# Attention layers of a transformer kernel: the large projection pieces in two halves, the small pieces behind the products with v

## The chip, the cores and the metric

One core of one Trainium2 chip runs the whole kernel. The metric is the device time of one execution in microseconds (us); the kernel before takes 1481.46 us, the median of three runs (1475.09 to 1482.32).

## The reference

The reference is two layers on x of shape (8, 512, 256). Layer one is softmax attention with 16 heads of 16, biases and a head mask, a residual and a layer norm. Layer two is a pre-norm block (rms norm, rotary embedding, causal attention, residual; rms norm, a mixture of 8 experts with the top 2 of each token, residual) with a residual and a layer norm around it.

```python
attn = softmax(einsum('bqhd,bkhd->bhqk', q, k) / sqrt(16)) * head_mask      # layer 1
x = layernorm(x + einsum('bhqk,bhkd->bqhd', attn, v).reshape(b, s, 256) @ Wo.T + bo)
h = x + causal_attention(rope(rmsnorm(x, g1)))                              # layer 2
y = h + moe(rmsnorm(h, g2))                                                 # 8 experts, top 2
x = layernorm(x + y)
```

## The kernel before

The change lies in `attention_layers`, which takes about the first 890 of the 1478 us. What follows it (routing, expert tiles, the last norm) is untouched.

**Units, groups, quarters.** Both attention layers run as one pipeline of 16 units u: units 0 to 7 ("plain") are the eight batches of layer one, units 8 to 15 ("causal") those of layer two. A unit has four groups n = 4u + g of four heads, and every group has four quarters (here q0 to q3; g0 to g3 for the groups). There are lead-in and run-out groups before and after (`FIRST` to `LAST`). Every engine walks the same loop over n and quarter in an order written out by hand; semaphores alone hold them together.

**A quarter on TensorE** (the loop at the end of the tensor block): two score products (`score`, tile `ps_s`, keys by queries of group n) and two products for the row maxima (`maximum`, tile `ps_m`, of group n + 3), then one *piece*, then two more of each, and then the product of the exponentials with v (`weigh`, tile `ps_o`). In causal units a masked diagonal (`diagonals`, L843 and the 128-column products behind it) follows the piece. `ps_s` and `ps_m` have three banks each: a product waits until ScalarE's exponential (`exponential`, L987) or VectorE's maximum (`take`, L1056) three back has emptied its bank.

**Pieces.** All other work of TensorE goes through the one bank `ps_x`. The table `piece_at(n, i)` names the piece that quarter i of group n carries. Eight of a unit are large: q and k of unit u + 2 (`qk`, four pieces in g1 and g3; six matmuls of 512 columns each, L670), v of unit u + 1 (two, g0; twelve of 256 columns, L681) and the output projection of unit u - 1 (`out`, two, g2; twelve of 256, L714). The small ones are `rows` (the maxima turned by four transposes, L702; two a unit) and, for causal units, `turn` (x, eight transposes, two), `parts` (the normed x, eight transposes, two) and `logits` (the router, 24 tiny matmuls). A piece waits until the previous one has been copied out of `ps_x` (`piece_out`). ScalarE copies out qk (`a_q`, L914, L917), v (L925), rows (L933) and the first half of turn and parts (L938, L944), between its exponentials; VectorE copies the second halves (L1117, L1124), the logits (L1130), and adds the residual to the output projection (L1141, L1146).

**What hangs on the pieces in causal units.** When the second qk piece of a half unit h is in `q32`, SyncE issues four DMAs that swap its rows for the rotary embedding (`swap`, L368); GpSimd multiplies them by sine, VectorE sums, GpSimd splits into two fp16 parts (`split_high`, `split_low`), SyncE stores them (`store_qk`, L373) and loads them back in the layout of the products (`load_qk`, L388, six DMAs). SyncE issues all DMAs of this stage in one order. At an even n it is:

```python
swap((n + 6) // 2)          # waits: emptied_piece(sync, "qk", h // 2, 2 * (h % 2) + 1)
load_qk((n + 4) // 2)       # waits: stored; its half unit is needed from the start of group n + 1
if g == 0: store_part(u - 3); load_res(u - 1)
else: load_x(u + 3)
store_o(n - 1)              # then stores and loads of expert weights
load_o(n // 2 - 1)
```

There are 16 swaps, at n = 26, 28, ..., 56. The first maxima that need what `load_qk` at n brings are those of group n + 4, which TensorE computes from the start of group n + 1 (`free_maximum` waits for `qk_loaded`). In plain units there is no swap; there GpSimd waits for the qk piece, in `split_high`.

## Time and profile before

| | |
|---|---|
| median of three runs | 1481.46 us |
| the profiled execution | 1479.55 us, its span 1477.6 us |
| TensorE matmuls busy | 1279.7 us (87%) |
| VectorE busy | 949.5 us (64%) |
| ScalarE busy | 829.9 us (56%) |
| GpSimd busy | 801.2 us (54%) |
| granted TensorE clock, mean | 0.939 of full speed |

The shares are means over stages with different limits: in the attention layers, the first 60% of the span, all engines are far busier than this, and TensorE shows 9 tenths and more in nearly every slice. A matmul's printed duration holds the time to its last result, so consecutive ones overlap; what TensorE spends is read from start to start. "Idle before" names the engine whose event ended a wait.

### The profile page before, as it was taken

To read this page: it belongs to the slowest core of one execution; us is meant where nothing else is said; L and a number is where in the kernel's file an instruction comes from. 1 tells how busy PE (TensorE), PEld (TensorE's weight loads), DVE (VectorE), ACT (ScalarE), POOL (GpSimd) and SP (SyncE) were. 2 spreads that over 40 slices of the span, in tenths; PEclk is the share of its full clock that TensorE was granted. 3 is DMA by queue.
4 is the path that set the end of the run, shared out by engine and by line. 5 is a ranking of instruction groups with operands and counts; after the bars stand their busy time and mean duration, and the time that the engine had idled before them with its cause. 6 is when DMAs were issued, how large, how long until landed. Compare 5 with 4: busy or idle time off the path is not lost. (4 is left out here: it accounts for less than half of the span.)

```text
span 1477.6 us, 33278 instructions
## 1 busy us (share of the span) xinstructions
PE 1279.7 (87%) x11533; PEld 712.1 (48%) x11534; DVE 949.5 (64%) x1766; ACT 829.9 (56%) x1672; POOL 801.2 (54%) x834
## 2 busy tenths in 40 slices
PE   1699999999999999999999963389999999999980
PEld 0222222232323444444444432378888888888870
DVE  6378888888898887977888613834444444444433
ACT  4148787888888776666676741133444344333334
POOL 2322565475546566765564333056666666666643
PEclk9769999999999999999999975589999999999995
DMA  4416767676767878887775534693222222222326
GB/s 127 86 36 171 179 180 200 188 197 201 196 178 216 216 224 210 234 217 207 166 190 156 132 95 129 178 261 61 43 43 44 45 46 43 43 43 44 42 29 235
DMA packets 158365, 204.21 MB, mean 138 GB/s; under 512 B 31088, under 2 KB 120688, under 8 KB 158256
## 3 DMA queue, kind: packets, MB, share of 16 engines
q1 hardware_dynamic: 140784, 182.29, 45.3%
q0 software_dynamic: 17472, 20.50, 8.9%
q8 instruction: 64, 1.05, 0.3%
q14 instruction: 45, 0.37, 0.1%
HBM read 111.20 MB, written 82.87 MB: 131 GB/s over the span
## 5 line engine op out<-in xcount | busy, mean ns | idle before, releaser
L987 ACT ACTIVATE a_probs<-a_ps_s 128x512 f32<-128x512 f32 (+2 forms) x896 | 460.0, 569 | 159.4 <-PE a_ps_s L782 154.3
L1056 DVE TENSOR_REDUCE a_shift_max<-a_ps_m 128x1 f16<-128x512 f32 x512 | 320.4, 682 | 70.5 <-PE a_ps_m L787 69.1
L787 PE MATMUL a_ps_m<-a_qkx 48*128 48x128 f16 (+3 forms) x1408 | 284.3, 301 | 21.1 <-DMA a_qkx<-a_qk_dram 8.9
L1606 PE MATMUL e_ps_gu<-e_xT,w_up 128*128 128x256 f16 x2574 | 297.8, 273 | 2.6 <-ACT e_xT L1661 2.4
L782 PE MATMUL a_ps_s<-a_qkx 49*128 49x128 f16 (+3 forms) x1408 | 275.4, 295 | 15.3 <-ACT a_probs L987 15.3
L1606 PEld LDWEIGHTS e_ps_gu<-e_xT,w_up 128*128 x2574 | 249.3, 98 | 36.1 <-issue 7.1
L883 PE MATMUL a_ps_o<-a_probs,a_v_one 128*32 128x512 f32 (+3 forms) x2048 | 234.1, 530 | 2.8 <-ACT a_o L994 2.7
L782 PEld LDWEIGHTS a_ps_s<-a_qkx 49*128 49x128 f16 x1408 | 89.6, 94 | 266.9 <-ACT a_probs L987 155.8
L1552 POOL DMA_INDIRECT h<-e_y,e_put x78 | 124.8, 1600 | 90.2 <-DVE e_y L1697 60.2
L1628 PE MATMUL e_ps_y<-w_down,e_h 128*128 x1404 | 162.7, 273 | 7.6 <-issue 5.0
L552 POOL TENSOR_TENSOR a_o_half<-a_o_half,a_inv_half 128x512 f32<-128x512 f32 x32 | 40.6, 1270 | 227.4 <-DMA a_inv_half<-a_inv_dram 227.4
L1709 DVE TENSOR_TENSOR e_h<-e_gate,e_ps_gu 128x512 f32<-128x512 f32 (+2 forms) x156 | 82.6, 550 | 126.2 <-ACT e_gate L1669 87.3
L1669 ACT ACTIVATE e_gate<-e_ps_gu 128x512 f32<-128x512 f32 x78 | 46.6, 597 | 200.9 <-PE e_ps_gu L1606 128.8
L1628 PEld LDWEIGHTS e_ps_y<-w_down,e_h 128*128 128x128 f16 x1404 | 127.9, 97 | 40.1 <-issue 14.9
L1056 DVE TENSOR_REDUCE a_neg_off<-a_ps_m 128x1 f32<-128x384 f32 (+2 forms) x256 | 138.1, 543 | 8.9 <-PE a_ps_m L787 8.1
L1715 DVE TENSOR_TENSOR e_h<-e_h 128x512 f16<-128x512 f32 (+2 forms) x156 | 83.5, 556 | 89.1 <-ACT e_h L1673 46.2
L539 POOL CAST a_qk<-a_q 128x1024 f16<-128x1024 f32 x32 | 33.2, 1036 | 157.6 <-DVE a_q L1111 96.0
L670 PE MATMUL a_ps_x<-a_xT,w_proj 128*128 128x512 f16 x384 | 101.6, 404 | 18.3 <-POOL a_xT L520 15.8
L787 PEld LDWEIGHTS a_ps_m<-a_qkx 48*128 48x128 f16 x1408 | 84.1, 94 | 63.9 <-DVE a_shift_max L1056 36.7
L1056 DVE TENSOR_REDUCE a_neg_max<-a_ps_m 128x4 f32<-128x512 f32 x128 | 87.7, 685 | 41.0 <-PE a_ps_m L787 40.2
L1564 POOL DMA_INDIRECT e_share<-weights,e_find x78 | 81.2, 1041 | 42.2 <-issue 42.2
L1538 POOL DMA_INDIRECT e_x<-part,e_take x78 | 81.2, 1041 | 41.5 <-issue 40.3
(195 smaller groups left out, 1661.0 us busy)
## 6 DMA issues: line engine op xcount, KB each, us to landing
a_qkx<-a_qk_dram SPq DMA_DIRECT2D x192, 128.0 KB, 4.5
a_qk_dram<-a_qk SPq DMA_DIRECT2D x32, 512.0 KB, 5.4
a_o_dram<-a_o SPq DMA_DIRECT2D x64, 256.0 KB, 2.7
a_o_half<-a_o_dram SPq DMA_DIRECT2D x32, 256.0 KB
a_inv_half<-a_inv_dram SPq DMA_DIRECT2D x32, 256.0 KB
part<-a_part SPq DMA_DIRECT2D x16, 512.0 KB, 5.8
a_q_swap<-a_q SPq DMA_DIRECT2D x64, 128.0 KB, 3.9
a_w_in<-in_wg SPq DMA_DIRECT2D x16, 352.0 KB, 5.4
```

What stands on the lines that cost most here:

```text
L670: mm = pe.matmul(ps_x[:], t.w_proj[:, 4 * layer + w, wh, k, m * P:(m + 1) * P], xT[:, u % 2, xh, k, :], start=n == 0, stop=n == 5)
L782: return pe.matmul(out, kx[first:first + 49, r, pair, kt * P:(kt + 1) * P], qx[first:first + 49, r, pair, q0:q1], start=start, stop=stop)
L787: return pe.matmul(out, qx[first:first + 48, r, pair, q * P:(q + 1) * P], kx[first:first + 48, r, pair, k0:k1], start=start, stop=stop)
L883: mm = pe.matmul(ps_o[32 * j:32 * (j + 1), S - w:S], v_one[:, u % 2, kt, g * HG + j, :], probs[:, kt // 2, j, first:first + w], start=kt = ...
L987: act.activation(dst, src, ACT.Exp).then_inc(exp_out, 1)
L1056: vector.tensor_reduce(out, src, AX.X, ALU.max, negate=True).then_inc(max_out, 1)
L1538: pool.indirect_dma_start(x[:, s, half], None, t.part_dram, bass.IndirectOffsetOnAxis(ap=take[:, s, half:half + 1], axis=0)).then_inc(gath ...
L1552: pool.indirect_dma_start(t.h_dram, bass.IndirectOffsetOnAxis(ap=put[:, s, half:half + 1], axis=0), y[:, s, half], None, compute_op=ALU.ad ...
L1606: mm = pe.matmul(ps_gu[:, bank, kind, f % 2], w[:, ds(e, 1)].rearrange("p o f -> p (o f)"), xT[:, s, xh, k, :], start=n == 0, stop=n == 5)
L1628: mm = pe.matmul(ps_y[:, s, half], h[:, s, hh, f, half * P:(half + 1) * P], w[:, ds(e, 1)].rearrange("p o f -> p (o f)"), start=c == 0, st ...
L1709: op = vector.tensor_tensor(h32[0:rows, bank, m], gate[0:rows, bank, m], ps_gu[0:rows, bank, 1, m], ALU.mult)
L1715: op = vector.tensor_tensor(h[0:rows, s, 1, f], h32[0:rows, bank, m], h[0:rows, s, 0, f], ALU.subtract)
```

## The change

Each large piece is cut into two halves of three matmuls of 512 columns, or six of 256, in two quarters that follow each other: piece (n, 2) in q2 and q3 of group n, and piece (n, 3) in q0 and q1 of group n + 1. Before, they stood whole in q2 and in q3 of group n. So every quarter now carries half a large piece at the place where the whole one stood. The small pieces move behind `weigh` at the end of q1 (piece (n, 0)) and of q3 (piece (n, 1)); the table swaps `parts` and `rows` in g1 and g3 so that `rows` stays in q1. ScalarE and VectorE copy out a large piece in q3 (of n) or q1 (of n + 1), after their second score or maximum (ScalarE after the first in q3 of causal units), and a small one at the very start of the next quarter. No instruction of the computation is added or taken away, and SyncE's and GpSimd's orders in the attention layers stay as they were.

```diff
@@ -243,16 +243,16 @@
         u, g = n // G, n % G
         kind, v, k = {
             (0, 0): ("turn", u + 2, 0), (0, 1): ("turn", u + 2, 1), (0, 2): ("v", u + 1, 0), (0, 3): ("v", u + 1, 1),
-            (1, 0): ("parts", u - 3, 1), (1, 1): ("rows", u, 1), (1, 2): ("qk", u + 2, 0), (1, 3): ("qk", u + 2, 1),
+            (1, 0): ("rows", u, 1), (1, 1): ("parts", u - 3, 1), (1, 2): ("qk", u + 2, 0), (1, 3): ("qk", u + 2, 1),
             (2, 0): ("logits", u - 3, 0), (2, 2): ("out", u - 1, 0), (2, 3): ("out", u - 1, 1),
-            (3, 0): ("parts", u - 2, 0), (3, 1): ("rows", u + 1, 0), (3, 2): ("qk", u + 2, 2),
+            (3, 0): ("rows", u + 1, 0), (3, 1): ("parts", u - 2, 0), (3, 2): ("qk", u + 2, 2),
             (3, 3): ("qk", u + 2, 3)}.get((g, i), (None, 0, 0))
         there = causal(v) if kind in ("turn", "logits", "parts") else unit(v)
         return (kind, v, k) if kind and there else None
...
     numbers = {}
     for n in range(FIRST, LAST):
-        for i in range(4):
+        for i in (0, 2, 1, 3):
             if piece_at(n, i):
                 numbers[piece_at(n, i)] = len(numbers)
...
-            def project(u, c):
+            def project(u, c, j):
 
                 layer = u // B
-                if plain(u):
-                    pe.wait_ge(xT_hi, u + 1)
-                    pe.wait_ge(xT_lo, u + 1)
-                else:
-                    emptied_piece(pe, "turn", u, 1)
+                if j == 0:
+                    if plain(u):
+                        pe.wait_ge(xT_hi, u + 1)
+                        pe.wait_ge(xT_lo, u + 1)
+                    else:
+                        emptied_piece(pe, "turn", u, 1)
                 w, m = c % 2, c // 2
-                n = 0
-                for wh, xh in ((0, 0), (0, 1), (1, 0)):
+                products = [(wh, xh, k) for wh, xh in ((0, 0), (0, 1), (1, 0)) for k in range(KD)]
+                for n in range(3 * j, 3 * j + 3):
+                    wh, xh, k = products[n]
+                    mm = pe.matmul(ps_x[:], t.w_proj[:, 4 * layer + w, wh, k, m * P:(m + 1) * P],
+                                   xT[:, u % 2, xh, k, :], start=n == 0, stop=n == 5)
+                if j == 1:
+                    piece_done(mm, "qk", u, c)
...
+            def project_v(u, i, j):
+                layer = u // B
+                n, q = 0, 2 * i + j
+                for wh, xh in ((0, 0), (1, 0), (0, 1)):
                     for k in range(KD):
-                        mm = pe.matmul(ps_x[:], t.w_proj[:, 4 * layer + w, wh, k, m * P:(m + 1) * P],
-                                       xT[:, u % 2, xh, k, :], start=n == 0, stop=n == 5)
+                        mm = pe.matmul(ps_x[:, j * D:(j + 1) * D], xT[:, u % 2, xh, k, q * P:(q + 1) * P],
+                                       t.w_proj[:, 4 * layer + 2, wh, k, :], start=n == 0, stop=n == 5)
                         n += 1
-                piece_done(mm, "qk", u, c)
...
+                if j == 1:
+                    piece_done(mm, "v", u, i)
...
+            def project_out(u, i, j):
                 layer = u // B
...
+                if j == 0:
+                    pe.wait_ge(aT_hi, 2 * u + 2)
+                    pe.wait_ge(aT_lo, 2 * u + 2)
...
+                if j == 1:
+                    piece_done(mm, "out", u, i)
...
-            def a_piece(n, i):
-                piece = piece_at(n, i)
+            def free_piece(piece):
+                if numbers[piece] > 0:
+                    pe.wait_ge(piece_out, numbers[piece])
+
+            def half_piece(n, quarter):
+
+                j = quarter % 2
+                piece = piece_at(n, 2) if quarter >= 2 else piece_at(n - 1, 3)
                 if piece is None:
                     return
                 kind, u, k = piece
-                if numbers[piece] > 0:
-                    pe.wait_ge(piece_out, numbers[piece])
+                if j == 0:
+                    free_piece(piece)
                 if kind == "qk":
-                    project(u, k)
+                    project(u, k, j)
                 elif kind == "v":
-                    project_v(u, k)
-                elif kind == "turn":
+                    project_v(u, k, j)
+                else:
+                    project_out(u, k, j)
+
+            def light_piece(n, quarter):
...
+
+                piece = piece_at(n, quarter // 2) if quarter % 2 else None
+                if piece is None:
+                    return
+                kind, u, k = piece
+                free_piece(piece)
+                if kind == "turn":
                     turn_x(u, k)
                 elif kind == "rows":
                     turn_maxima(u, k)
-                elif kind == "out":
...
@@ -891,7 +907,7 @@
                         maximum(n + 3, quarter, i)
                         if i == 0:
                             causal_maximum(n + 3, quarter, 0)
-                    a_piece(n, quarter)
+                    half_piece(n, quarter)
                     diagonals(n, n + 3, quarter)
                     for i in range(2, 4):
                         score(n, quarter, i)
@@ -902,6 +918,7 @@
                         weigh(n - 1, 2 + quarter)
                     else:
                         weigh(n, quarter - 2)
+                    light_piece(n, quarter)
...
-            def empty_piece(n, i):
-                piece = piece_at(n, i)
+            def empty_piece(n, quarter):
+                piece = piece_at(n, 2) if quarter == 3 else piece_at(n - 1, 3) if quarter == 1 else None
...
+            def empty_light(n, quarter):
+                piece = piece_at(n, 0) if quarter == 2 else piece_at(n - 1, 1) if quarter == 0 else None
+                if piece is None:
+                    return
+                kind, u, k = piece
+                if kind == "rows":
                     move_rows(u, k)
...
                 for quarter in range(4):
-                    early = (1 if quarter < 2 else 0) if causal(u) else 3
+                    early = 0 if causal(u) and quarter >= 2 else 1
+                    empty_light(n, quarter)
                     for i in range(4):
...
             def empty_piece(n, quarter):
+                if n % G == 2 and quarter == 3:
+                    residual(n // G - 1, 0)
+                elif n % G == 3 and quarter == 1:
+                    residual(n // G - 1, 1)
+
+            def empty_light(n, quarter):
                 u, g = n // G, n % G
-                if g == 0 and quarter == 1:
+                if g == 1 and quarter == 0:
                     move_x(u + 2)
-                elif g == 1 and quarter == 0:
+                elif g == 2 and quarter == 0:
                     move_parts(u - 3)
-                elif g == 2 and quarter == 0:
+                elif g == 2 and quarter == 2:
                     move_logits(u - 3)
-                elif g == 2 and quarter >= 2:
-                    residual(u - 1, quarter - 2)
...
                 for quarter in range(4):
-                    early = causal((n + 3) // G)
+                    empty_light(n, quarter)
                     for i in range(4):
                         row_max(n + 3, quarter, i)
                         if i < 3:
                             causal_row_max(n + 3, quarter, i)
-                        if i == (0 if early else 3):
+                        if i == 1:
                             empty_piece(n, quarter)
```

TensorE in a plain unit, from the transposes of `rows` in g1 q1 to the next qk piece; S is `a_ps_s`, the maxima `a_ps_m`, the product with v `a_ps_o`. Before:

```order
L702 MATMUL a_ps_x<-ident,a_shift_max 8x128 x4
L782 MATMUL a_ps_s<-a_qkx 128x512
L787 MATMUL a_ps_m<-a_qkx 128x512
L782 MATMUL a_ps_s<-a_qkx 128x512
L787 MATMUL a_ps_m<-a_qkx 128x512
L883 MATMUL a_ps_o<-a_probs,a_v_one 32x512 x4
L782 MATMUL a_ps_s<-a_qkx 128x512
L787 MATMUL a_ps_m<-a_qkx 128x512
L782 MATMUL a_ps_s<-a_qkx 128x512
L787 MATMUL a_ps_m<-a_qkx 128x512
L670 MATMUL a_ps_x<-a_xT,w_proj 128x512 x6
```

Now, the same stretch:

```order
L899 MATMUL a_ps_o<-a_probs,a_v_one 32x512 x4
L703 MATMUL a_ps_x<-ident,a_shift_max 8x128 x4
L798 MATMUL a_ps_s<-a_qkx 128x512
L803 MATMUL a_ps_m<-a_qkx 128x512
L798 MATMUL a_ps_s<-a_qkx 128x512
L803 MATMUL a_ps_m<-a_qkx 128x512
L671 MATMUL a_ps_x<-a_xT,w_proj 128x512 x3
L798 MATMUL a_ps_s<-a_qkx 128x512
L803 MATMUL a_ps_m<-a_qkx 128x512
L798 MATMUL a_ps_s<-a_qkx 128x512
L803 MATMUL a_ps_m<-a_qkx 128x512
L899 MATMUL a_ps_o<-a_probs,a_v_one 32x512 x4
```

The transposes have moved from the middle of the quarter to its end, where two scores and two maxima part them from the next large piece (before, four of each and a product with v), and only three of the six matmuls of that piece stand in this quarter.

ScalarE in a causal unit, the copies of the last two qk pieces of a unit (`a_q`); the second is what the swap waits for. Before, from g3 q2 on (both copies are in g3, and q0 of the next unit's g0 begins with the `128x384 x2`):

```order
L914 ACTIVATE a_q<-a_ps_x 128x512
L987 ACTIVATE a_probs<-a_ps_s 128x2x2x128
L1002 ACTIVATE a_squares,a_ms<-a_hid 128x256
L987 ACTIVATE a_probs<-a_ps_s 128x2x128
L914 ACTIVATE a_q<-a_ps_x 128x512
L987 ACTIVATE a_probs<-a_ps_s 128x2x2x128
L1002 ACTIVATE a_squares,a_ms<-a_hid 128x256
L987 ACTIVATE a_probs<-a_ps_s 128x384 x2
```

Now, from g3 q3 on:

```order
L931 ACTIVATE a_q<-a_ps_x 128x512
L1010 ACTIVATE a_probs<-a_ps_s 128x2x2x128
L1025 ACTIVATE a_squares,a_ms<-a_hid 128x256
L961 ACTIVATE a_nT<-a_ps_x 128x1024
L1010 ACTIVATE a_probs<-a_ps_s 128x384 x2
L1010 ACTIVATE a_probs<-a_ps_s 128x2x2x128
L1010 ACTIVATE a_probs<-a_ps_s 128x384 x2
L1010 ACTIVATE a_probs<-a_ps_s 128x2x256
L931 ACTIVATE a_q<-a_ps_x 128x512
```

The second copy has moved by two quarters, from q3 of a group to q1 of the next, behind six exponentials of that next group; and a copy of a small piece (`a_nT`) opens the group.

## Rows read from the trace of the kernel before

**Rows 1.** Busy time by stretch: a plain and a causal stretch of 100 us.
```profile
core 0: us, PE busy (x) PEld busy (x) DVE busy (x) ACT busy (x) POOL busy (x), PEclk, DMA share, GB/s
300.00:400.00 100.00, 94.24 (x680) 28.91 (x673) 88.86 (x161) 85.76 (x168) 58.47 (x59) 1.00 0.72 195
700.00:800.00 100.00, 98.49 (x1190) 46.19 (x1185) 83.82 (x149) 69.92 (x153) 58.51 (x45) 1.00 0.72 174
```

**Rows 2.** Busy time by stretch: the groups g0, g1, g2, g3 of one plain unit.
```profile
291.80:303.96 12.16, 11.17 (x84) 3.94 (x82) 10.47 (x21) 9.22 (x19) 11.14 (x15) 1.00 0.84 202
303.96:316.10 12.14, 11.89 (x84) 3.12 (x81) 10.24 (x18) 11.62 (x24) 7.95 (x6) 1.00 0.56 188
316.10:329.00 12.90, 11.64 (x94) 4.12 (x92) 10.81 (x19) 11.20 (x23) 10.61 (x9) 1.00 0.86 204
329.00:342.40 13.40, 12.81 (x86) 3.30 (x82) 13.11 (x27) 10.74 (x22) 0.00 (x0) 1.00 0.58 183
```

**Rows 3.** Instructions in order, TensorE, plain: start, duration, engine, line, operation.
```profile
309.08 0.39 PE L782 MATMUL a_ps_s<-a_qkx 49*128 49x512 f16 x1
...
309.62 1.47 PE L670 MATMUL a_ps_x<-a_xT,w_proj 128*128 128x512 f16 x6
311.02 0.39 PE L782 MATMUL a_ps_s<-a_qkx 49*128 49x512 f16 x1
...
312.56 0.39 PE L782 MATMUL a_ps_s<-a_qkx 49*128 49x512 f16 x1
...
319.00 0.39 PE L782 MATMUL a_ps_s<-a_qkx 49*128 49x512 f16 x1
...
321.52 0.39 PE L782 MATMUL a_ps_s<-a_qkx 49*128 49x512 f16 x1
```

**Rows 4.** The same view, causal: TensorE from g1 q3 to g3 q0.
```profile
717.99 1.47 PE L670 MATMUL a_ps_x<-a_xT,w_proj 128*128 128x512 f16 x6
...
721.00 0.33 PE L782 MATMUL a_ps_s<-a_qkx 49*128 49x384 f16 x1
...
723.58 0.33 PE L782 MATMUL a_ps_s<-a_qkx 49*128 49x384 f16 x1
...
733.07 0.33 PE L782 MATMUL a_ps_s<-a_qkx 49*128 49x384 f16 x1
```

**Rows 5.** The same view, ScalarE: the copy that the swap waits for.
```profile
719.49 0.60 ACT L914 ACTIVATE a_q<-a_ps_x 128x512 f32<-128x512 f32 x1 [1.02 <-PE a_ps_x L670]
```

**Rows 6.** The same view, SyncE's DMA issues around it.
```profile
720.12 3.10 SPq L368 DMA_DIRECT2D a_q_swap<-a_q  x4
724.06 2.66 SPq L388 DMA_DIRECT2D a_qkx<-a_qk_dram  x6
```

**Rows 7.** Another load (SyncE), and when TensorE, waiting for it, went on.
```profile
551.36 3.62 SPq L388 DMA_DIRECT2D a_qkx<-a_qk_dram  x6
...
559.03 0.39 PE L787 MATMUL a_ps_m<-a_qkx 48*128 48x256 f16 x2 [0.66 <-DMA a_qkx<-a_qk_dram]
```

**Rows 8.** Tile a_qkx, 697 to 745 us: time from a DMA's issue to landing.
```profile
DMA to landing us min/median/max: 3.2/4.6/6.3
```

**Rows 9.** TensorE after two waits, causal units.
```profile
631.37 2.74 PE L714 MATMUL a_ps_x<-w_proj,a_aT 128*128 128x256 f16 x12 [2.08 <-DVE a_hid L1146]
...
683.31 1.48 PE L714 MATMUL a_ps_x<-w_proj,a_aT 128*128 128x256 f16 x12 [2.10 <-DVE a_hid L1146]
```

**Rows 10.** Groups by line and form, 560 to 800 us: copies of small pieces.
```profile
L933 ACT ACTIVATE a_rows<-a_ps_x 8x512 f16<-8x512 f16 x10 | 5.7, 569 | 0.0
...
L944 ACT ACTIVATE a_nT<-a_ps_x 128x1024 f16<-128x1024 f16 x4 | 4.1, 1024 | 0.0
...
L1124 DVE COPY a_nT<-a_ps_x 128x1024 f16<-128x1024 f16 x3 | 2.1, 686 | 0.0
```

**Rows 11.** Who waited for whom, TensorE, 500 to 700 us.
```profile
PE a_ps_x L714 <- DVE a_hid L1146: 4.2, 2, 2.1
PE a_ps_x L714 <- POOL a_aT L558: 3.0, 4, 0.9
```

More of the change, by code:

```diff
@@ L672, in project @@
                         n += 1
-                piece_done(mm, "qk", u, c)
-            def project_v(u, i):
-                layer = u // B
-                for j in range(2):
-                    n, q = 0, 2 * i + j
-                    for wh, xh in ((0, 0), (1, 0), (0, 1)):
-                        for k in range(KD):
-                            mm = pe.matmul(ps_x[:, j * D:(j + 1) * D], xT[:, u % 2, xh, k, q * P:(q + 1) * P],
-                                           t.w_proj[:, 4 * layer + 2, wh, k, :], start=n == 0, stop=n == 5)
-                            n += 1
-                piece_done(mm, "v", u, i)
+                if j == 1:
+                    piece_done(mm, "v", u, i)
@@ L704, in turn_maxima @@
                 piece_done(mm, "rows", u, c)
-            def project_out(u, i):
+            def project_out(u, i, j):
                 layer = u // B
-                pe.wait_ge(aT_hi, 2 * u + 2)
-                pe.wait_ge(aT_lo, 2 * u + 2)
-                for j in range(2):
-                    n, q = 0, 2 * i + j
-                    for wh, ah in ((0, 0), (1, 0), (0, 1)):
-                        for k in range(KD):
-                            mm = pe.matmul(ps_x[:, j * D:(j + 1) * D], aT[:, u % 2, ah, k, q * P:(q + 1) * P],
-                                           t.w_proj[:, 4 * layer + 3, wh, k, :], start=n == 0, stop=n == 5)
-                            n += 1
-                piece_done(mm, "out", u, i)
+                if j == 0:
+                    pe.wait_ge(aT_hi, 2 * u + 2)
+                    pe.wait_ge(aT_lo, 2 * u + 2)
+                n, q = 0, 2 * i + j
+                for wh, ah in ((0, 0), (1, 0), (0, 1)):
+                    for k in range(KD):
+                        mm = pe.matmul(ps_x[:, j * D:(j + 1) * D], aT[:, u % 2, ah, k, q * P:(q + 1) * P],
+                                       t.w_proj[:, 4 * layer + 3, wh, k, :], start=n == 0, stop=n == 5)
+                        n += 1
+                if j == 1:
+                    piece_done(mm, "out", u, i)
             def turn_parts(u, hl):
@@ L752, in a_piece @@
                     turn_maxima(u, k)
-                elif kind == "out":
-                    project_out(u, k)
                 elif kind == "parts":
@@ L954, in empty_piece @@
                     move_v(u, k)
-                elif kind == "rows":
+            def empty_light(n, quarter):
[4 more added lines that the diff above has]
+                if kind == "rows":
                     move_rows(u, k)
```

## The prediction

> **What bounds the kernel now.** The change touches only the attention layers, so I read the busy time by stretch first. In plain units three engines are nearly full at once (of 100 us TensorE 94, VectorE 89, ScalarE 86); in causal units TensorE alone is (98.5; VectorE 84, ScalarE 70) [rows 1]. Within one plain unit the limit moves with the group: ScalarE is busy 11.62 of 12.14 us in g1 (it has the layer norm there), VectorE 13.11 of 13.40 in g3 (statistics, low parts), neither in g0 and g2 [rows 2].
>
> Then the instructions in order. A plain quarter with a large piece takes TensorE 3.48 us (309.08 to 312.56), 1.40 of it the piece (309.62 to 311.02), so 2.08 without; yet a quarter without a large piece lasts 2.52 us (319.00 to 321.52) [rows 3], because there TensorE waits for the four exponentials and four maxima. That is the unevenness on which an evening-out can earn. In causal units the same piece costs as much and there is next to no waiting to fill [rows 1, 4].
>
> Last, what hangs on the pieces. The copy of the second qk piece ends at 720.09 [rows 5], SyncE issues the swap at 720.12 and is done with it at 723.22, and at 724.06 starts the load of qkx [rows 6], which TensorE needs at 733.07, at the start of g3 [rows 4]. So from copy to need there are 13.0 us today, and the chain uses most of them.
>
> **Halves, in plain units.** Every quarter gets half a piece: half of 1.40 is 0.70, and each piece has one seam more. A seam costs nothing if the next matmul overlaps as before, and at most what a lone matmul shows over its pitch, 0.39 against 1.40/6 = 0.23, so 0 to 0.16 us; I take 0.10. A quarter is then 2.08 + 0.75 = 2.83 us on TensorE, a group 11.3. By groups: g0 11.3 (was 12.16), g1 11.8 (ScalarE's 11.6 busy binds; was 12.14), g2 11.4 (was 12.90), g3 13.8 (was 13.40: VectorE is full, and gets the second residual, about 0.6 us, out of g2) [rows 2]. Sum 48.3 against 50.6. With three banks the engines cannot even out everything, so of the 2.3 I take 1.2 us a unit, over 7 steady units -8 us; ends 0 and -16.
>
> **Halves, in causal units.** TensorE is full, so an evening-out earns nothing there and the seams are paid: 8 units of 8 pieces, 64 x 0.10 = +6 us (0 to +10).
>
> **The late copy, and SyncE behind it.** This is the term that decides. The second qk piece of a half unit ends two quarters later, in q1 of the next, even group. SyncE's order is unchanged, so at that even n it now stands at `swap` until q1, and behind the swap are queued: the load of qkx, the store of parts or load of x, the store of o, the weights, the load of o. The load is waited for by TensorE itself. Worked out on the same place: TensorE reaches g2 q1 at 723.58 [rows 4] (half a piece more in q0, but the logits, now behind q1, less), passes two scores and maxima in 0.54 (309.08 to 309.62) and the half in 0.75 [rows 3], so 724.9; the copy of 0.60 [rows 5] makes it 725.5 instead of 720.09. To 733.07 there would be 7.6 us; q2 and q3 hold one large piece instead of two (-1.4), the logits come behind (+0.7), a little of waiting goes or comes: 6.5 to 7.6, I take 7.3. The chain: 3.10 for the four issues of the swap, then the load. From its first issue to TensorE going on I have 7.67 us where TensorE did wait (551.36 to 559.03) [rows 7]; from the median landing, 5/6 of 2.66 for the last issue plus 4.6, it is 6.8 [rows 6, 8]. The part that waits today for the stored qk (0.84 us between swap and load) is gone. So 3.1 + 6.8 = 9.9 against 7.3: a stall of 2.6 us at the first maximum of g1 and g3. With the fastest landing (3.2) it is 8.5 against 7.6, 0.9 us; with the 7.67 it is 10.8 against 6.5, 4.3 us. I take 2.6, near the median landing. There are 16 swaps: +42 us (+14 to +69).
>
> The rest of the queue is late by the same 3 to 5 us (the load of o, VectorE's reciprocal, GpSimd's normalising, the out piece), but TensorE comes later to its need by the stall, so I cost it at nothing; without that cover it would be some 2 us a unit, which the heavy case below holds. In plain units GpSimd, not SyncE, waits for the late copy; it shows no busy time at all in g3 [rows 2], so a later start at an even group is made up there: nothing.
>
> The Trainium skill ("DMA: Bandwidth & Descriptors", section "Anatomy of one DMA — SWDGE (gpsimd) path") puts a transfer at about 2.0 us and its bytes at 436 GB/s, which for the 0.79 MB of the six loads would be an estimated 3.8 us from the first issue, 6.9 with the swap, and no stall at all; the trace does not agree, its fastest single landing of 128 KB is 3.2 us and the median 4.6 [rows 8], in a stage where the DMA engines are 0.72 busy [rows 1].
>
> **What the stall does to the clock.** After 2.08 us of idling a piece of twelve took 2.74 us, the length it has at 1.2 GHz; after 2.10 us another took 1.48, that of 2.4 GHz [rows 9]. So a stall of this size costs 1.26 us more or nothing. I take a quarter of the cases, 16 x 0.3 = +5 us (0 to +20).
>
> **Small pieces behind the product with v.** Until now the next piece came a whole quarter later and the copy had time. Now only two scores and maxima (0.54 us) lie between a small piece and the next large half, which waits for the copy. ScalarE's copy of rows is 0.57 us: with the signals 0.15 each, twice a unit. Its copy of parts is 1.02: 0.55, once. VectorE's copy is 0.69 and often stands behind other work: 0.45, once [rows 10]. The two of x fall inside the load's cover or beside its stall and cost nothing of their own; the logits' copy is short. 1.3 us a unit, over 8 causal units +10 (0 to +20). In plain units only rows is left, about 2 us, inside the spread of the first term.
>
> **Waits that go.** TensorE waited 4.2 us for the residual and 3.0 for `a_aT` between 500 and 700 us [rows 11], and once ran at half clock behind it. The residual is now a quarter later and what feeds it the same: -6 us (0 to -10).
>
> **Sum.** -8 + 6 + 42 + 5 + 10 - 6 = +49 us. The profiled execution took 1479.55 us (span 1477.6), so 1528.6; the median of the runs shown lies 1.9 above it, so **1530 us**.
>
> **Rivals.** (1) *The load lands fast*, since it no longer shares the DMA engines with the store of qk just before it: stall 0.9 us, no clock loss: -8 + 6 + 14 + 10 - 6 = +16, 1497 us. For it: the 3.2 us landing. Against: everything behind the swap is issued in one burst. (2) *Evening-out wins*: the swap's lateness stays inside the cover, and all of the plain gain is had: -16 + 3 + 0 + 2 - 10 = -21, 1460 us, faster. Its place is the first maximum of g1 and g3, and it decides if copy to landing takes no more than 7.6 us. For it: the 0.96 us by which a light quarter is shorter than a heavy one now. Against: the shortest chain that I can build from rows is 8.5. (3) *No stall, but the small things stay*, as the page's rule would have it: -8 + 6 + 0 + 10 - 6 = +2, 1483 us. The chain would have to shrink as in (2). (4) *Heavy*: stalls of 4.3 us with half clock after each: -8 + 6 + 69 + 20 + 10 - 6 = +91, 1572 us; TensorE shows 7.67 us of load where it was congested [rows 7], and that was with weights still moving.
>
> **Chances.** Forecast 0.50, (1) 0.18, (2) 0.14, (3) 0.09, (4) 0.09. No change means within 0.5%, about 7 us, which is what a measurement of this kernel can tell. Slower is the forecast, (1) and (4): 0.77; same is (3): 0.09; faster is (2): 0.14. The range reaches from just below (3) to the near side of (4), 1478 to 1562 us, and leaves out (2) and most of (4), 0.2.
>
> **What would show it.** Right: in causal groups the qkx load is issued some 4 us later within its group, TensorE's list of waits has `a_qkx` with 16 waits and about 40 us instead of a few, always at the start of g1 and g3; plain units shorten to about 49.4 us; half clock in some causal slices. The small pieces show as waits of the next half for `a_nT`, `a_rows`. Wrong: if waits for `a_qkx` sum to under 10 us the main term is gone, and the time lies at (2) or (3); if a plain unit stays at 50.6 or grows, the three banks do not let the engines even out; if plain units fall to 48 the gain was undersized.

## The result, and the profile after

The changed kernel takes 1574.82 us (median of 4 runs, 1572.63 to 1582.2), the kernel before 1478.28 on the same chip. The ratio is 1.066, 95% interval 1.061 to 1.072: 96 us slower. The forecast was 1530 with a range to 1562, so the sign was right and the size short by 45 us. The profiled execution took 1572.94 us, its span 1571.0.

The page of the changed kernel has one group that stands out (section 5: busy time and mean ns of one, then the idle time before and what ended most of it):

```profile
L803 PE MATMUL a_ps_m<-a_qkx 48*128 48x128 f16 (+3 forms) x1408 | 291.1, 315 | 71.5 <-DMA a_qkx<-a_qk_dram 65.0
```

In the kernel before the same line (L787 there) showed 21.1 us of idle time and 8.9 for the load. Busy time by stretch, the same two stretches as in [rows 1]:

```profile
core 0: us, PE busy (x) PEld busy (x) DVE busy (x) ACT busy (x) POOL busy (x), PEclk, DMA share, GB/s
300.00:400.00 100.00, 93.70 (x652) 25.07 (x652) 87.41 (x155) 82.70 (x163) 56.82 (x58) 0.98 0.68 193
700.00:800.00 100.00, 88.45 (x922) 38.13 (x922) 65.98 (x115) 55.28 (x112) 53.89 (x41) 0.86 0.62 160
```

The plain stretch hardly moved; the causal one does 922 matmuls where it did 1190, and the granted clock fell from 1.00 to 0.86.

The period of a unit, read from the start of its first v piece to that of the next unit's, tells where the time went (periods are read from the profiled execution of each kernel). Units 1 to 5 (plain) last 51.9 us on average instead of 50.6. Units 6 to 13, in which the late swaps fall, last 60.3 instead of 49.4: 8 x 10.8 = +86.5 us. From the v piece carried in unit 0 to the one in unit 14 it is +89.4 in all. The very first v piece, in the lead-in, starts 1.1 us sooner.

**A late load, step by step.** These rows answer to [rows 4 to 6]. They are of unit 10, where the wait is one of the longest; the place that the prediction worked out, unit 12, follows behind them. TensorE from q1 of g2 to g3 (start, duration, instruction; in brackets what it waited for):

```profile
667.59 0.82 PE L671 MATMUL a_ps_x<-a_xT,w_proj 128*128 128x512 f16 x3
...
669.59 0.23 PE L798 MATMUL a_ps_s<-a_qkx 49*128 49x128 f16 x1
...
672.63 0.23 PE L798 MATMUL a_ps_s<-a_qkx 49*128 49x128 f16 x1
...
675.22 0.33 PE L798 MATMUL a_ps_s<-a_qkx 49*128 49x384 f16 x1
680.46 0.60 PE L803 MATMUL a_ps_m<-a_qkx 48*128 48x256 f16 x2 [4.91 <-DMA a_qkx<-a_qk_dram]
680.86 0.52 PE L798 MATMUL a_ps_s<-a_qkx 49*128 49x384 f16 x1
681.32 1.46 PE L715 MATMUL a_ps_x<-w_proj,a_aT 128*128 128x256 f16 x6
...
685.15 0.50 PE L798 MATMUL a_ps_s<-a_qkx 49*128 49x384 f16 x1
...
685.86 0.83 PE L715 MATMUL a_ps_x<-w_proj,a_aT 128*128 128x256 f16 x6
```

ScalarE's copy in the same place, and SyncE's issues:

```profile
669.07 0.62 ACT L931 ACTIVATE a_q<-a_ps_x 128x512 f32<-128x512 f32 x1
```
```profile
669.72 2.48 SPq L368 DMA_DIRECT2D a_q_swap<-a_q  x4
672.29 2.85 SPq L388 DMA_DIRECT2D a_qkx<-a_qk_dram  x6
```

The copy ends at 669.69, the swap is issued 0.03 us later, the load 2.57 us after that, and TensorE goes on at 680.46. The chain took 10.8 us from the end of the copy. From there to TensorE's need (675.22 and the 0.33 us of one score) it was 5.9 us, nearly all of it q2 and q3 (669.59 to 675.22). The rest is a stall of 4.9 us. Behind it TensorE is at the lower level of its clock: six matmuls print 1.46 us there and 0.83 in the next quarter, at 685.86.

At the worked-out place, in unit 12, the same rows (ScalarE, SyncE, TensorE) are:

```profile
792.26 0.62 ACT L931 ACTIVATE a_q<-a_ps_x 128x512 f32<-128x512 f32 x1
```
```profile
792.90 2.47 SPq L368 DMA_DIRECT2D a_q_swap<-a_q  x4
795.47 4.31 SPq L388 DMA_DIRECT2D a_qkx<-a_qk_dram  x6
```
```profile
794.47 1.22 PE L715 MATMUL a_ps_x<-w_proj,a_aT 128*128 128x256 f16 x6 [0.56 <-DVE logits L1154]
...
804.31 0.39 PE L803 MATMUL a_ps_m<-a_qkx 48*128 48x256 f16 x2 [2.80 <-DMA a_qkx<-a_qk_dram]
```

Here the chain took 11.4 us and the stall 2.8, so the time to the need was 8.6. It is longer than in unit 10 mostly because TensorE itself was slower: it has the logits' piece, which unit 10 has not, it waited for their copy, and the half piece behind that wait prints 1.22 us instead of 0.83. Over the 15 late loads for which TensorE waited between 420 and 900 us, the chain took 10.0 to 11.8 us (10.8 in the mean), the time to the need was 5.9 to 9.0 (7.8) and the stall 1.0 to 5.0 (3.0). From the first issue of the load to TensorE going on it was 7.2 to 9.2 us (7.9).

TensorE's list of waits, 420 to 900 us (us in total, times, longest):

```profile
PE a_ps_m L803 <- DMA a_qkx<-a_qk_dram: 44.6, 15, 5.0
PE a_ps_x L671 <- ACT a_rows L950: 6.2, 14, 0.7
PE a_ps_x L681 <- ACT a_xT L955: 5.9, 7, 0.9
PE a_ps_x L703 <- DVE a_hid L1170: 3.7, 5, 0.8
PE a_ps_x L715 <- DVE logits L1154: 2.9, 3, 1.5
PE a_ps_x L671 <- ACT a_nT L961: 2.5, 4, 0.6
```

In the kernel before the first of these is 2.5 us in 4 waits for the same stretch. Four of the others are large halves that wait until a small piece (`rows`, x, the logits, the normed x) has been copied out: 17.5 us in 28 waits. The fifth, L703, is the small piece `rows`, which waits for VectorE's residual.

**Plain units.** TensorE in unit 4, which answers to [rows 3]:

```profile
309.31 0.82 PE L671 MATMUL a_ps_x<-a_xT,w_proj 128*128 128x512 f16 x3 [0.32 <-ACT a_rows L950]
...
312.14 0.82 PE L671 MATMUL a_ps_x<-a_xT,w_proj 128*128 128x512 f16 x3
...
314.97 0.82 PE L671 MATMUL a_ps_x<-a_xT,w_proj 128*128 128x512 f16 x3
...
317.80 0.82 PE L671 MATMUL a_ps_x<-a_xT,w_proj 128*128 128x512 f16 x3
...
321.94 0.81 PE L715 MATMUL a_ps_x<-w_proj,a_aT 128*128 128x256 f16 x6 [1.24 <-POOL a_aT L558]
...
329.29 0.39 PE L803 MATMUL a_ps_m<-a_qkx 48*128 48x512 f16 x2 [1.84 <-DMA a_qkx<-a_qk_dram]
```

The quarters last 2.83 us, to the hundredth what the forecast worked out, and the time won is then waited away: 11.3 us for `a_qkx` in 8 waits between 100 and 350 us, against 0.5 before. The 9.0 us for which TensorE waited there for ScalarE's exponentials before are down to 0.9.

### The profile page after: what moved, and what is told of

It reads as the page before. It is cut to its first block and busy times, and to the rows that moved or that the text cites. A ratio compares the mean times of both kernels' runs of the same rounds, so it can differ in the third digit from the quotient of the medians.

```text
span 1571.0 us, 33278 instructions
## 1 busy us (share of the span) xinstructions
PE 1319.7 (84%) x11533; PEld 706.8 (45%) x11534; DVE 953.1 (61%) x1766; ACT 839.5 (53%) x1672; POOL 803.3 (51%) x834
## 5 line engine op out<-in xcount | busy, mean ns | idle before, releaser
L1010 ACT ACTIVATE a_probs<-a_ps_s 128x512 f32<-128x512 f32 (+2 forms) x896 | 467.0, 566 | 252.7 <-PE a_ps_s L798 248.0
L1080 DVE TENSOR_REDUCE a_shift_max<-a_ps_m 128x1 f16<-128x512 f32 x512 | 324.9, 685 | 71.4 <-PE a_ps_m L803 70.7
L803 PE MATMUL a_ps_m<-a_qkx 48*128 48x128 f16 (+3 forms) x1408 | 291.1, 315 | 71.5 <-DMA a_qkx<-a_qk_dram 65.0
L798 PE MATMUL a_ps_s<-a_qkx 49*128 49x128 f16 (+3 forms) x1408 | 289.6, 307 | 2.3 <-ACT a_probs L1010 2.3
L899 PE MATMUL a_ps_o<-a_probs,a_v_one 128*32 128x512 f32 (+3 forms) x2048 | 244.1, 551 | 3.4 <-ACT a_o L1017 3.3
L1080 DVE TENSOR_REDUCE a_neg_off<-a_ps_m 128x1 f32<-128x384 f32 (+2 forms) x256 | 139.2, 545 | 49.8 <-PE a_ps_m L803 49.3
L671 PE MATMUL a_ps_x<-a_xT,w_proj 128*128 128x512 f16 x384 | 110.8, 401 | 30.7 <-POOL a_xT L520 15.9
```

The costliest lines, as they stand in the source:

```text
L671: mm = pe.matmul(ps_x[:], t.w_proj[:, 4 * layer + w, wh, k, m * P:(m + 1) * P], xT[:, u % 2, xh, k, :], start=n == 0, stop=n == 5)
L798: return pe.matmul(out, kx[first:first + 49, r, pair, kt * P:(kt + 1) * P], qx[first:first + 49, r, pair, q0:q1], start=start, stop=stop)
L803: return pe.matmul(out, qx[first:first + 48, r, pair, q * P:(q + 1) * P], kx[first:first + 48, r, pair, k0:k1], start=start, stop=stop)
L899: mm = pe.matmul(ps_o[32 * j:32 * (j + 1), S - w:S], v_one[:, u % 2, kt, g * HG + j, :], probs[:, kt // 2, j, first:first + w], start=kt = ...
L1010: act.activation(dst, src, ACT.Exp).then_inc(exp_out, 1)
L1080: vector.tensor_reduce(out, src, AX.X, ALU.max, negate=True).then_inc(max_out, 1)
```

## The experiments

Each ran beside the kernel before, whose median was 1478.9 to 1480.4 us. Differences are from that median; ratios have 95% intervals. Edits are shown in part; `...` marks what is left out. The changed kernel is "changed", the one before "before".

**1. The load ahead of the swap.** Changed, SyncE at even n:

```diff
-                    swap((n + 6) // 2)
                     load_qk((n + 4) // 2)
+                    swap((n + 6) // 2)
```

> The changed kernel with one thing moved: on SyncE the load of qkx now stands ahead of the swap at even n, so that the load no longer waits for the late copy. Theory A (the load held behind the swap is what costs: 65 us of waits for a_qkx and the half clock after them): 1480 to 1505 us, waits of TensorE for a_qkx down from 65 us to under 20, mean clock back to about 0.94. Rival B (the halves and the small pieces themselves cost, and the late load only shows up in the list of waits): still over 1545 us, the waits reappear at other places (a_nT, a_rows, a_xT, a_hid).

Measured: 1531.9 us, ratio 1.034 (1.028 to 1.040). That is 43 us less than changed, and TensorE's waits for `a_qkx` fall from 65.0 to 20.4 us, but 52 us of the loss stay. Neither expectation held: the load behind the swap is a large part, and not the whole. GpSimd, which waits 15.0 us in 7 places for the swapped rows in changed (420 to 900 us), waits 78.1 us in 16 here; experiment 11 takes that up.

**2. The lateness alone, without halves.** Before, with the swap made to wait until the end of q1's exponentials:

```diff
                     if k > 0:
                         sync.wait_ge(rope_out, 2 * k)
+                    sync.wait_ge(exp_out, items(2 * h - 6) + 6)
```

> The kernel before, whole pieces in their old places, with one wait added: at even n SyncE issues the swap only when ScalarE has done six exponentials of group n, about where the changed kernel's copy ends. Theory A: this alone gives most of the loss, 1535 to 1575 us, with waits for a_qkx of 3 to 5 us at the start of g1 and g3 and a mean clock near 0.91. It has one whole piece more between swap and need than the changed kernel (1.4 us), so each stall should be about 1.4 us shorter than there. Rival B: under 1500 us.

Measured: 1556.2 us, ratio 1.051 (1.044 to 1.057). Pieces, copies and everything else are as in before, and still 76 us are lost. TensorE, 420 to 900 us:

```profile
PE a_ps_m L788 <- DMA a_qkx<-a_qk_dram: 42.7, 16, 4.9
```

It waits 16 times and 42.7 us, nearly what changed shows. Against before, with 8.9 us over the whole span, that is 34 us more of waiting, and yet 76 are lost: each microsecond of stall costs about two. VectorE does not wait for `a_q_swap` here. The granted clock accounts for the rest; 420 to 880 us in before, in changed and in this run (columns as above):

```profile
420.00:880.00 460.00, 431.93 (x4708) 187.92 (x4700) 353.81 (x631) 320.15 (x684) 262.58 (x220) 0.98 0.71 190
420.00:880.00 460.00, 392.84 (x3804) 156.98 (x3802) 307.08 (x547) 272.77 (x559) 229.75 (x194) 0.90 0.64 167
420.00:880.00 460.00, 409.27 (x3881) 169.05 (x3877) 310.21 (x553) 274.89 (x562) 230.52 (x197) 0.86 0.65 167
```

The clock is either at its full or at half its level, so a mean of 0.86 says that it was low for some 130 of these 460 us (2 x 0.14 x 460, an estimate), against 18 in before and 92 in changed. What low time costs can be read off one quarter: from the half piece to the next score it lasts 3.8 us behind the stall in changed (681.32 to 685.15) and 2.2 at full clock in experiment 1 (655.04 to 657.20), so about 44% of low time is lost. That makes an estimated 49 us here, and with the 34 us of waiting 83 against 76 measured.

**3. The small pieces alone.** Before, with the small pieces behind `weigh` of q1 and q3 and copied out at the start of the next quarter (ScalarE's and VectorE's part of the edit is not shown); large pieces whole, in q2 and q3:

```diff
-                    a_piece(n, quarter)
+                    if quarter >= 2:
+                        a_piece(n, quarter)
...
                         weigh(n, quarter - 2)
+                    if quarter % 2:
+                        a_piece(n, quarter // 2)
```

> The kernel before with whole large pieces in q2 and q3 as they were, and only the small pieces moved behind the product with v, copied out at the start of the next quarter. SyncE's swap keeps its time. Theory A: the small pieces cost about 10 us, 1483 to 1500 us. Rival B (small pieces are a main cost, since the next piece waits for their copy): over 1520 us.

Measured: 1502.1 us, ratio 1.015 (1.010 to 1.019): +22 us where the prediction had +10. Units 1 to 5 last 51.7 us instead of 50.6 and units 6 to 13 51.3 instead of 49.4, that is about +5 and +15.

**4. Keeping TensorE busy in the stall.** Changed, with twelve matmuls of 512 columns (their results unused) ahead of each of 16 waits for the load:

```diff
+                if number >= 3:
+                    pe.wait_ge(max_out, number - 2)
+                if number == items(n) and n % 2 == 0 and 30 <= n <= 60:
+                    for _ in range(12):
+                        pe.matmul(ps_m[:, number % 3], t.w_proj[:, 0, 0, 0, 0:P], ..., start=True, stop=True)
                 if number == items(n):
                     pe.wait_ge(qk_loaded[h % 4], 96 * (h // 4 + 1))
-                if number >= 3:
-                    pe.wait_ge(max_out, number - 2)
```

> The changed kernel with twelve matmuls of 512 columns put in front of TensorE's wait for a_qkx at the 16 starts of g1 and g3 where a swap precedes the load (about 2.6 us of work that nothing uses). If the half clock after the stalls is a cost of its own, TensorE stays at full speed and the time falls by 20 to 45 us, to 1530 to 1555, though work was added. If the stalls alone cost, the time stays at 1575 or rises by up to 10 us, since some stalls are shorter than 2.6 us.

Measured: 1563.2 us, ratio 1.055 (1.050 to 1.059), 11.6 less than changed, whose interval (1.061 to 1.072) it does not touch, with 192 matmuls more; the granted clock is 0.97 to 1.00 in each 100 us from 420 to 880 us, where changed has 0.86 to 0.93. It fell outside both expectations' numbers. TensorE's time at these places did not shrink: the remaining waits for `a_qkx` are 7.2 us (420 to 900 us), and the filler takes 2.76 us at each of 16 places, 51 us together against 44.6. So what was won came from the clock, and it is at least 12 us. By the reckoning of experiment 2 the low clock costs changed some 30 us more than before (92 us low against 18, at 44%). That is an estimate; it is more than the 12 because the filler itself adds 7 us and the waits for small pieces grow.

**5. The swap last.** Experiment 1, with the swap moved on, behind `load_o`:

```diff
                     load_qk((n + 4) // 2)
-                    swap((n + 6) // 2)
...
                     load_o(n // 2 - 1)
+                    swap((n + 6) // 2)
```

> The changed kernel with SyncE's order at an even n altered: load_qk first, then the stores and loads of that group (part or x, o, expert weights, load_o), and swap last. With swap directly behind load_qk the time was 1532, 52 us above the kernel before; the small pieces behind weigh alone cost 22. Theory A (everything that stood behind the waiting swap was late: the store of o, the reciprocals, a_aT): 1500 to 1512, about what the small pieces cost. Rival B (halves themselves cost in the causal units: seams, copies nearer to the next piece's wait): stays 1525 to 1540. Rival C (a late swap also delays the chain of the rotary embedding): above 1540.

Measured: 1645.2 us, ratio 1.114 (1.109 to 1.118). Rival C, and far more of it than I had thought. Units 6 to 13 last 69.2 us. GpSimd, in order, stands waiting for the swapped rows, and VectorE, in order, for GpSimd's product. VectorE's waits (640 to 880 us), and TensorE's for VectorE (700 to 900 us):

```profile
DVE a_q L1135 <- POOL a_q_swap L528: 52.2, 7, 9.2
```
```profile
PE a_ps_x L703 <- DVE a_hid L1170: 23.6, 3, 9.8
PE a_ps_m L803 <- DVE a_neg_off L1080: 21.6, 4, 8.9
```

So the swap has two customers. One is the load queued behind it, the other the chain swap, sine (GpSimd), sum (VectorE, `rope_sum` in q0 of the odd group), which holds up VectorE's maxima when it is late.

**6. The store of qk earlier as well.** Experiment 5, and in odd groups:

```diff
                 else:
+                    early = plain((n + 5) // 4)
+                    if early:
+                        store_qk((n + 5) // 2)
                     load_rows((n + 1) // 2)
...
                     load_inv((n - 3) // 2)
+                    if not early:
+                        store_qk((n + 5) // 2)
                     for m in weights_at(n - 1):
...
-                    store_qk((n + 5) // 2)
```

> e5_swap_last, and in odd groups store_qk stands earlier in SyncE's order: in plain units first in the group, in causal units directly behind load_inv, ahead of the expert weights. In the changed kernel a plain unit lasts 51 to 53 us although its quarters run at 2.83 us (45.3 a unit), and TensorE waits for a_qkx at the start of odd groups (0.8 to 2.4 us). Theory A (the evening-out is there, and SyncE's in-order chain of store_qk, its landing and load_qk hides it): no a_qkx waits in plain units, a plain unit falls to 47 to 49.5 us, the whole 12 to 30 us below e5. Rival B (VectorE and ScalarE bind the plain unit as a whole): plain units stay above 50 and the total is within 8 us of e5.

Measured: 1615.6 us, ratio 1.093 (1.088 to 1.098), 30 us under experiment 5. Units 1 to 5 last 49.3 us, against 52.2 in experiment 5, 51.9 in changed and 50.6 in before. This is theory A: the evening-out is there once the store leaves early. It accounts for half of the 30 us (5 x 2.9). Most of the other half is in units 6 to 13 (66.8 us instead of 69.2), where the store has moved as well, ahead of the expert weights; no run shows why it pays there.

**7. The early store alone.** Before, with the diff of experiment 6.

> The kernel before with the same earlier store_qk and nothing else. If SyncE's chain binds plain units of the kernel before as well (their period is 50.0 to 51.1 us), it gets faster, 1455 to 1472. If only halved pieces reach the bound of that chain, as I think, it stays within 7 us of the kernel before: 1473 to 1487.

Measured: 1479.4 us, ratio 1.001 (0.999 to 1.004). No change, as expected: with whole pieces the load was not late in plain units.

**8. Halves made whole again.** Experiment 5, with both halves in the first of the two quarters, copied out there:

```diff
-                if j == 0:
-                    free_piece(piece)
-                if kind == "qk":
-                    project(u, k, j)
+                if j == 1:
+                    return
+                free_piece(piece)
+                for j in range(2):
+                    if kind == "qk":
+                        project(u, k, j)
...
```

> e5_swap_last with large pieces whole again: piece (n, 2) whole in q2 of n, piece (n, 3) whole in q0 of n + 1, each copied out in its own quarter; small pieces and SyncE's order as in e5. It tells what halving does by itself. Theory A (halving evens out nothing that pays, since other chains set the unit): within 8 us of e5. Rival B (halving pays in plain units): 10 to 20 us slower than e5. Rival C (seams and late copies of halves cost in the causal units): 8 to 20 us faster than e5.

Measured: 1638.2 us, 7 below experiment 5, inside theory A's bound. Both copies and the swap's release come a quarter earlier here, so the 7 us are not the price of halving alone; but halving by itself is not where tens of microseconds go.

**9. and 10. Halves in plain units only.** Changed up to q1 of group 23, from there on the layout of before; experiment 9 has the early store of experiment 6 too, experiment 10 has not.

```diff
+    halves = lambda n, quarter: 4 * n + quarter < 4 * 23 + 2
...
-                    half_piece(n, quarter)
+                    if halves(n, quarter):
+                        half_piece(n, quarter)
+                    else:
+                        whole_piece(n, quarter)
```

> Halves only in plain units, up to q1 of group 23; from q2 of group 23 on everything stands as in the kernel before (whole pieces, small pieces in their old places), and there is no late swap in causal units. SyncE has the early store_qk of e6 (plain units: first in odd groups; causal: behind load_inv). Theory A (evening-out earns 1.3 us a unit once SyncE's store is early, and nothing of the loss arises in plain units): 5 to 6 units x 1.3 = 7 to 10 us under the kernel before, 1468 to 1475. Rival B (the 1.3 us were noise of one profile): 1477 to 1486.

> The same halves only in plain units, with SyncE's order as in the kernel before. Theory A (the load of qkx is late by SyncE's order, the quarters' gain is waited away): 1480 to 1489. Rival B (halves earn in plain units as they are, and everything lost is lost in causal units): 1468 to 1476.

Measured: experiment 9 takes 1472.0 us, ratio 0.9939 (0.9914 to 0.9963); experiment 10 1477.7, ratio 0.9988 (0.9975 to 1.0001). Units 1 to 5 last 48.9 us with the early store and 51.2 without. SyncE around one load, in experiment 10 and in experiment 9:

```profile
311.65 0.64 SPq L435 DMA_DIRECT2D a_inv_half<-a_inv_dram  x1
...
313.79 0.46 SPq L380 DMA_DIRECT2D a_qk_dram<-a_qk  x1
318.74 2.65 SPq L395 DMA_DIRECT2D a_qkx<-a_qk_dram  x6
```
```profile
302.84 0.64 SPq L435 DMA_DIRECT2D a_inv_half<-a_inv_dram  x1
...
305.04 2.74 SPq L395 DMA_DIRECT2D a_qkx<-a_qk_dram  x6
```

and TensorE's waits for it, 100 to 350 us, in the same order:

```profile
PE a_ps_m L824 <- DMA a_qkx<-a_qk_dram: 9.9, 8, 2.6
```
```profile
PE a_ps_m L828 <- DMA a_qkx<-a_qk_dram: 1.2, 2, 0.8
```

From the issue of `a_inv_half` to the load it is 7.1 us in the one and 2.2 in the other, where the store (313.79 in experiment 10) no longer has to leave and land between them. Experiment 9 beats both kernels, by 0.6% against before.

**11. The load ahead of the swap, in before.** The diff of experiment 1 on before.

> The kernel before with load_qk ahead of swap at even n, nothing else. There TensorE waits 8.9 us for a_qkx in all, and the swap is issued about 3 us later. If a late swap costs by itself (VectorE's rope_sum waits for GpSimd's a_q_swap, as in e5 where it waited 52 us in 7 places), it is slower than before by 3 to 15 us; if it has room at this place, 1471 to 1482.

Measured: 1505.7 us, ratio 1.017 (1.015 to 1.020): +27 us, nearly twice the most that was expected. A swap issued behind the load instead of ahead of it is enough. GpSimd's product and VectorE's sum in one place:

```profile
729.79 2.68 POOL L528 TENSOR_TENSOR a_q_swap<-a_q_swap,rope_sin 128x512 f32<-128x512 f32 x2 [2.76 <-DMA a_q_swap<-a_q]
732.57 0.69 DVE L1111 TENSOR_TENSOR a_q<-a_q_cos,a_q_swap 128x512 f32<-128x512 f32 x1 [1.23 <-POOL a_q_swap L528]
```

and the lists of waits between 560 and 860 us:

```profile
POOL a_q_swap L528 <- DMA a_q_swap<-a_q: 46.4, 11, 6.5
DVE a_q L1111 <- POOL a_q_swap L528: 6.8, 6, 1.4
```

In before neither of these two waits occurs between 560 and 860 us. TensorE's waits for `a_neg_off` grow from 3.3 to 15.1 us (420 to 900 us), and the mean clock is 0.919 in this profile, against 0.939. Units 6 to 13 last 52.5 us instead of 49.4, +24 us.

**12. Both repairs of changed.** Experiments 1 and 6 together, the swap directly behind the load.

> The changed kernel with load_qk ahead of swap, and store_qk early as in e6. From e1_load_first (1532) the plain units should give back 2 us each, some 12 to 14 us: 1512 to 1522. What then stays over the kernel before, some 35 to 40 us, is the causal units: 22 as in e3_small_alone, the rest waits behind the late copy. If it stays at 1526 or more, the early store earns nothing where the load is not last.

Measured: 1505.4 us, ratio 1.016 (1.013 to 1.019). The early store gives back 26 us from experiment 1, more than expected: units 1 to 5 last 49.2 us instead of 52.0 (14 us), and from 420 to 900 us the waits for `a_qkx` go from 5.3 to 0.4. What is left over before is 26 us. That is near what experiment 3 found for the small pieces, but by coincidence: plain units are faster here than in before, and units 6 to 13 last 54.1 us instead of 49.4, +37 us, which is what the small pieces (+15 in experiment 3) and the swap behind the load (+24 in experiment 11) cost there together. The same two account for most of experiment 1, whose units 6 to 13 last 54.6 us, +42.

## Why the prediction was wrong in size

**What held.** The mechanism: the late copy holds SyncE at the swap and the load behind it, TensorE waits for `a_qkx` at the start of odd groups, and half clock follows. Experiment 2 has this by itself and loses 76 us. The half piece has a pitch of 0.75 us (312.14 to the next score at 312.89), as taken. The waits for the load come to what was forecast: +42 us, and 44.6 against 2.5 were measured. Halving costs 0.10 us a piece, as taken (twice 0.75 against 1.40), so the +6 for seams stands. The small pieces show as waits for `a_rows`, `a_nT` and their like.

**The failing step: what a stall does to the clock.** It was put at "a quarter of the cases, 16 x 0.3 = +5 us". Experiment 4 takes most of this away and wins 12 us with 192 matmuls more, so 12 us is the least. From the mean clock of 0.90 instead of 0.98 and the price read off one quarter it is about 30 us (experiment 2 has the working, an estimate). So the term is 12 to 30 us. I had taken both outcomes of [rows 9] for stalls of 2.1 us, at one in four and 1.26 us each. These stalls are up to 5.0 us long, one of them is followed by 3.8 us where 2.2 would do for the next quarter alone, and the waits for small pieces bring low clock as well: at 794.47 it follows a wait of 0.56 us for the logits. The Trainium skill ("TensorE: Matmul & The Clock Gate", section "HAM oscillation — how this bites in real kernels") describes a kernel that waits for a transfer in every tile and starts each tile slow; the row at 681.32 agrees.

**Small pieces: +10 forecast, +22 measured** (experiment 3), about 15 in causal units and 5 in plain ones. The copies were priced one by one, and x and the logits at nothing. In changed TensorE waits for x 5.9 us in 7 places, for the logits 2.9 in 3 and for `rows` 6.2 in 14 (0.44 each, where 0.15 was taken). The plain units pay 1.1 us each, where 2 us were taken for all of them.

**The stall: 2.6 us forecast, 3.0 measured as a mean, 5.0 at most.** The chain was 10.8 us in the mean instead of 9.9, and the time to the need 7.8 instead of 7.3, so two misses of the same sign nearly cancel; at the place worked out it was 11.4 against 8.6. The step that was short is the load: 6.8 us from its first issue to TensorE going on, worked out from the median landing of one DMA, where 7.9 was measured. TensorE needs the last of six, and [rows 7] had 7.67. The estimate of 3.8 us in the prediction, from the Trainium skill's section on transfers that GpSimd issues, took six transfers of SyncE as one; no load here took under 7.2. The total for `a_qkx` is 65.0 us against 8.9; some 11 of the difference is plain.

**Plain units: -8 forecast, about +2 measured.** Unit 0 got 3.4 us shorter and the first v piece starts 1.1 sooner, but units 1 to 5 got 1.3 us longer each. "In plain units GpSimd, not SyncE, waits for the late copy ... nothing" looked only at GpSimd. With shorter quarters SyncE's own order is the limit: `store_qk` stands last in an odd group, behind `load_inv` and the weights, and its landing separates it from the load. Experiments 6, 9 and 10 show it. With the store early a plain unit is 1.3 to 1.8 us shorter than before, close to the 1.2 that I had taken for the evening-out.

**The rest of the queue: nothing forecast.** SyncE's later swap is not free even where the load no longer waits for it. Experiments 5 and 11 show the second path, over GpSimd and VectorE. In changed it does not show: GpSimd waits there for the swapped rows (15.0 us in 7 places, 420 to 900 us), VectorE never for GpSimd. With the load put first it does: in experiment 1 GpSimd waits 78.1 us in 16 places and VectorE 6.7 in 5 for GpSimd, and that is part of why experiment 1 got back no more than 43 us. That TensorE's stalls are what gives this path its time in changed is argued; no run shows it by itself, and no run has halves in causal units with the swap on time.

Added up from these: plain +2 (its small pieces with it), seams +6, small pieces in causal units +15, waits for the load +42, clock +12 to +30, that is 77 to 95 against a difference of 93 between the two profiled executions. "Waits that go" (-6) is not seen as a gain of its own. So of the 44 us that were missing, up to 25 are the clock, 10 the plain units, 6 the waits that did not go and 5 the small pieces. The heavy rival (4), 1572 us, was nearest, at a chance of 0.09, and partly by luck: it took stalls of 4.3 us, where a mean of 3.0, plain units that gained nothing and dearer small pieces gave the same sum.

## What to carry over

When work is moved later, list everybody who is queued behind the engine that waits for it, and every in-order engine behind those; here one copy held a DMA queue, and by it a load, GpSimd and VectorE. Where an engine needs all parts of a transfer, take the chain from a place where it was seen to wait for them (7.67 us here), not from the median landing of one part (6.8). Price a stall of TensorE with what the clock takes behind it, and when one engine's quarters get shorter, look for the round trip through memory that now sets the pace: moving one store up made the same halves worth 0.6% instead of nothing.

## What the runs showed of the hardware

A microsecond of waiting for the load cost TensorE about two (experiment 2: 34 us more of waits, 76 us more of time, granted clock 0.86 instead of 0.98 from 420 to 880 us). Filling such waits with unused matmuls raised the granted clock from 0.90 to 0.98 over the same stretch and made the kernel 11.6 us faster (experiment 4). The chain of four DMA issues of 128 KB, six more, and the landing of the last took 10.8 us, of which 5.3 are the issues themselves (2.48 + 2.85 in unit 10).
